# Transposing a value matrix and ternary feed-forward weights on VectorE instead of TensorE, in a graph layer on one Trainium2 core

## What is computed

```
xn = layernorm(x)
x  = x + segment_sum((xn @ W)[src] * edge_weight, dst) + mix(xn)
mix: q, k, v = xn @ Wq.T + bq, xn @ Wk.T + bk, xn @ Wv.T + bv      # q, k divided by their norms
     s = sum over m of phi(q) * phi(k), per head;  out = s * v / s
x  = x + ffn(layernorm(x))
ffn: act_quant(x) @ weight_quant(w_gate).T, the same with w_up, silu(gate) * up, then w_down
weight_quant(w): scale = 1 / mean(|w|);  wq = clip(round(w * scale), -1, 1) / scale
```

## Time and profile before

| what | us |
|---|---|
| median of 3 runs | 1679.87 |
| lowest and highest run | 1676.17, 1680.43 |
| the profiled execution's own time | 1680.37 |
| its span on the core | 1678.6 |
| TensorE busy in it | 1653.2 |
| VectorE busy | 1095.4 |
| ScalarE busy | 519.1 |
| GpSimd busy | 588.5 |

### The profile page before, as it was taken

One profiled execution on the slowest core, in us unless ns is written; L12 is line 12 of the kernel. 1 busy time (PEld: TensorE's weight loads), 2 busy tenths in 40 slices (PEclk: granted clock), 3 DMA queues, 4 the chain that ended last, 5 costly groups with the idle time before them and its releaser, 6 DMA issues.

```text
span 1678.6 us, 23146 instructions
## 1 busy us (share of the span) xinstructions
PE 1653.2 (98%) x8036; PEld 1344.9 (80%) x8036; DVE 1095.4 (65%) x2548; ACT 519.1 (31%) x618; POOL 588.5 (35%) x392
## 2 busy tenths in 40 slices
PE   6999999999999999999999999999999999999998
PEld 5899999888888888888877777888788887887665
DVE  7866573576676876656666664476485674764886
ACT  4632210222222111114232222233333333332554
POOL 2011565777776777777677700000000000000000
PEclk9999999999999999999999999999999999999999
DMA  9999878655676755657877747345345345452454
GB/s 295 377 402 348 308 234 263 169 138 124 151 195 167 183 141 149 149 138 191 243 209 192 191 147 205 102 135 137 96 146 136 96 136 145 136 145 62 146 172 123
DMA packets 158003, 302.93 MB, mean 180 GB/s; under 512 B 60241, under 2 KB 95105, under 8 KB 157938
## 3 DMA queue, kind: packets, MB, share of 16 engines
q1 hardware_dynamic: 88302, 222.54, 42.2%
q0 software_dynamic: 61824, 52.62, 15.3%
q10 hardware_dynamic: 7812, 26.97, 5.3%
HBM read 202.88 MB, written 99.20 MB: 180 GB/s over the span
## 4 chain that ended last, share of the span: by engine, by line
PE 91%; DMA 5%; DVE 2%; issue 1%; ACT 1%; SPq 0%; DVEq 0%; ACTq 0%
PE PS L367 23%; PE PS L368 23%; PE PS L366 23%; PE PS L1408 4%; PE PS L1410 4%; PE PS L1409 4%; PE PS L1645 4%; DMA Aside<-A_dense 2%; PE PS L1675 2%; PE PS L1472 2%; DMA xnT<-XT 1%; DMA X<-in_x 1%; PE PS L1624 1%; DVE stats L995 1%; PE PS L1388 0%
## 5 line engine op out<-in xcount | busy, mean ns | idle before, releaser
L706 POOL DMA_INDIRECT A_dense<-wtot,cell x336 | 545.4, 1623 | 229.5 <-DMA A_dense<-wtot,cell 133.9
L367 PE MATMUL PS<-SH,AL 125*125 125x512 f32 x784 | 310.0, 395 | 0.0
L366 PE MATMUL PS<-SL,AH 125*125 125x512 f32 x784 | 308.4, 393 | 1.6 <-DVE AL L1222 1.4
L368 PE MATMUL PS<-SH,AH 125*125 125x512 f32 x784 | 309.8, 395 | 0.0
L366 PE MATMUL PS<-WL,xtH 128*125 128x512 f32 x640 | 252.9, 395 | 0.0
L367 PE MATMUL PS<-WH,xtL 128*125 128x512 f32 x640 | 252.0, 394 | 0.0
L368 PE MATMUL PS<-WH,xtH 128*125 128x512 f32 x640 | 251.6, 393 | 0.0
L1220 DVE TENSOR_TENSOR SL<-S,SH 125x1024 fp32r<-125x1024 f32 x98 | 119.9, 1223 | 166.1 <-ACT SH L895 166.1
L895 ACT ACTIVATE SH<-S 125x1024 fp32r (+1 forms) x98 | 103.9, 1061 | 316.4 <-PE PS L368 316.3
L366 PEld LDWEIGHTS PS<-SL,AH 125*125 125x125 f32 x784 | 145.9, 186 | 39.8 <-DVE AL L1222 3.1
L367 PEld LDWEIGHTS PS<-SH,AL 125*125 125x125 f32 x784 | 146.1, 186 | 36.0
(11 more groups left out here) (190 smaller groups left out, 2547.9 us busy)
## 6 DMA issues: line engine op xcount, KB each, us to landing
A_dense<-zeros POOLq DMA_DIRECT2D x40, 1280.0 KB, 8.3
xt<-xnT SPq DMA_DIRECT2D x60, 500.0 KB, 6.1
Araw<-A_dense SPq DMA_DIRECT2D x100, 250.0 KB, 2.7
Aside<-A_dense SPq DMA_DIRECT2D x100, 250.0 KB, 2.9
keyrow<-key_rows SPq DMA_DIRECT2D x42, 512.0 KB, 4.1
ewrow<-weight_rows SPq DMA_DIRECT2D x42, 512.0 KB, 5.6
xnT<-XT ACTq DMA_DIRECT2D x20, 500.0 KB, 10.2
zx<-in_x SPq DMA_DIRECT2D x20, 448.0 KB
```

Of the source, the lines that this page charges most:

```text
L366: nc.tensor.matmul(o, lh, rl, start=start, stop=False)
L367: nc.tensor.matmul(o, ll, rh, start=False, stop=False)
L368: return nc.tensor.matmul(o, lh, rh, start=False, stop=stop)
L706: pool.indirect_dma_start(cells[m], bass.IndirectOffsetOnAxis(cell[:, col:col + 1], 0), wtot[:, col:col + 1], None, compute_op=ALU.add).th ...
```

## The change

Two transposes leave TensorE. VectorE's transpose works on blocks of 32 by 32, so a 128 by 128 transpose needs the blocks put in their places as well; here the access pattern of the instruction and the store to DRAM do that.

- **Wv.** In map tiles 10 to 17 DVE turns one block of Wv at the end of the tile (`turn_blocks`, into one buffer `turned`), and SP stores it with four DMAs of 32 partitions. ACT's copy is gone. wvT now holds column blocks instead of k-blocks, so W can no longer be replaced block by block: in the last source tiles TensorE makes the left half of the columns of both tiles, then the right halves (`half_products`), and the first two value tiles go in the same order. ACT and DVE replace four column blocks at a time.
- **Ternary weights.** The twelve chunks are quantised in the aggregation's group 0 instead of the value stage, in the places given by CHUNKS_AT (pair h of source tiles). The sums of |w| stay where they were. POOL's queue loads the chunks and stores them, eight DMAs of 32 partitions each, after the scatter is over. DVE turns the rounded chunk. SP reads wT in group 1 instead of group 0.
- The feed-forward matmuls read wT in 16 runs of 32 columns.
- EDGE_PLAN moves four pairs of edge columns from the map stage into the stage of Wq's and Wk's Gram matrices, and the scatter leaves out the three columns that hold no edge (333 instead of 336).

```diff
-EDGE_PLAN = [1] * TILES + [0, 0, 0, 0, 1, 1, 1, 1] + [0, 1, 1, 0, 1, 1, 0, 1] + [1, 0, 1, 0, 1, 0, 1, 1] \
-    + [1, 1, 1, 1, 1, 1, 0, 0] + [4] + [2] * KT + [3] * (TILES - KT) + [4] * 18 + [0] * 2
+EDGE_PLAN = [1] * TILES + [0, 0, 0, 0, 1, 1, 1, 1] + [0, 1, 1, 1, 1, 1, 0, 1] + [1] * KT \
+    + [1, 1, 1, 1, 1, 1, 0, 0] + [4] + [2] * KT + [3, 3] + [3, 2] * (KT // 2) + [3, 3] + [4] * 18 + [0] * 2
...
+CHUNKS_AT = (0, 0, 1, 1, 2, 1, 2, 1, 2, 2)
...
+    def across_blocks(ap):
+        return ap.rearrange("p (k b j) -> p b k j", b=4, j=32), lambda o: o.rearrange("p (b k j) -> p b k j", b=4, j=32)
+
+    def turn_blocks(out_, in_):
+        order_in, order_out = across_blocks(in_)
+        return nc.vector.transpose(order_out(out_), order_in)
...
+    def store_halves(eng, dram, rows, sem, down):
+        for a in range(4):
+            for c in range(2):
...
+                eng.dma_start(to, rows[a * 32:(a + 1) * 32, :].rearrange("p (b c f) -> p b c f", b=4, c=2)[:, :, c]).then_inc(sem, 16)
...
@@ sync @@
-        for f in range(3):
-            load_next_A(f + 2)
+        for hh in range(2, HALF + 2):
+            load_next_A(hh)
+        for f in range(3):
+            for i in range(2):
+                sp.wait_ge(s_fout[i], 128 * (2 * f + 2))
             sp.dma_start(wT[:, f], wT_d[4 * f:4 * f + 4].rearrange("c p n -> p c n")).then_inc(s_wT, 16)
+            load_next_A(HALF + 2 + f)
@@ gpsimd, behind the scatter @@
+        wait_stage4(pool)
+        for i in range(2):
+            pool.wait_ge(s_pe5[i], 1)
+        for c in range(2):
+            load_chunk(c)
+        for c in range(12):
+            if c + 2 < 12:
+                pool.wait_ge(s_fq16[c % 2], c // 2 + 1)
+                load_chunk(c + 2)
+            pool.wait_ge(s_fT[c % 2], c // 2 + 1)
+            store_halves(pool, wT_d[c], gTb[:, c % 2, :], s_fout[c % 2], c >= 8)
@@ scalar, in group 0 behind both source tiles of pair h @@
+            for c in range(chunk, chunk + CHUNKS_AT[h]):
+                act.wait_ge(s_fr[c % 2], c // 2 + 1)
+                if c >= 2:
+                    act.wait_ge(s_fT[c % 2], c // 2)
+                nc.scalar.activation(gqb[:, c % 2, :], gwb[:, c % 2, :], ACT.Identity, bias=neg_round[:, :]).then_inc(s_fq16[c % 2], 1)
@@ vector, map stage @@
+            j = t - V_TURN
+            if 0 <= j < KT:
+                dve.wait_ge(s_stage[j % 2], 32 + 16 * (KT // 2) + 16 * (j // 2) + 16)
+                if j:
+                    dve.wait_ge(s_vout, 64 * j)
+                turn_blocks(turned[:, :], stage[:, j % 2, :]).then_inc(s_vtr, 1)
@@ vector, group 0 @@
+            low_of_sources(2 * h, 0, h)
+            for c in range(chunk, chunk + CHUNKS_AT[h]):
...
+            low_of_sources(2 * h + 1, 1, h)
+            for c in range(chunk, chunk + CHUNKS_AT[h]):
+                i = c % 2
+                dve.wait_ge(s_fq16[i], c // 2 + 1)
+                if c >= 2:
+                    dve.wait_ge(s_fout[i], c // 2 * 128)
+                turn_blocks(gTb[:, i, :], gqb[:, i, :]).then_inc(s_fT[i], 1)
@@ tensor @@
-                for e in range(8):
-                    last = nc.tensor.transpose(PS16[:, 6 + i, e * P:(e + 1) * P], fqb[:, i, e * P:(e + 1) * P], ident16[:, :])
-                last.then_inc(s_ftr[i], 1)
...
+        pe.wait_ge(s_vl, KT // 2)
+        for i in range(2):
+            pe.wait_ge(s_xtl[i], 2 * HALF + 1)
+            pe.wait_ge(s_supev[i], HALF)
+            half_products(i, 0)
+        pe.wait_ge(s_vl, KT)
+        for i in range(2):
+            half_products(i, 1).then_inc(s_mm[i], 1)
...
+        def up_blocks(c, k):
+            return wT[:, c, :, :].rearrange("p q (a k j) -> p (q a) k j", a=4, j=32)[:, :, k, :]
```

More of the change, by code:

```diff
@@ L94 @@
 END_AT = 229368
+CHUNKS_AT = (0, 0, 1, 1, 2, 1, 2, 1, 2, 2)
+assert len(CHUNKS_AT) == HALF and sum(CHUNKS_AT) == 12
 def split_rows(eng, dst, src, sem):
@@ L590, in stage4_tile @@
                 load_next_A(0)
-            if chunk is None and isinstance(h, int) and t < 6:
+            if t < 5:
                 for a in range(2):
@@ L703, in scatter_pair @@
             turns[m] += 1
-            for c in range(2):
-                col = 2 * pair + c
+            for col in range(2 * pair, min(2 * pair + 2, COLS)):
+                c = col % 2
                 pool.indirect_dma_start(cells[m], bass.IndirectOffsetOnAxis(cell[:, col:col + 1], 0),
@@ L861, in _ @@
         high_of_tile(1, HALF - 1 + PASS)
+        act.wait_ge(s_wk, 1)
+        for j in range(KT // 2):
+            high_of_block(j)
         sources_out(HALF - 1, 0)
         high_of_tile(0, HALF + PASS)
[L865 to L871 removed]
@@ L917, in _ @@
         act.wait_ge(s_mm[1], 3 * HALF)
-        with act.Fori(1, HALF) as h:
+        chunk = 0
+        for h in range(1, HALF):
             high_of_pair(0, h)
+            for c in range(chunk, chunk + CHUNKS_AT[h]):
[3 more added lines that the diff above has]
+                nc.scalar.activation(gqb[:, c % 2, :], gwb[:, c % 2, :], ACT.Identity, bias=neg_round[:, :]).then_inc(s_fq16[c % 2], 1)
+            chunk += CHUNKS_AT[h]
         def move_rows(g):
@@ L1287, in _ @@
         stage4_tile(9, 1)
-        with dve.Fori(1, HALF) as h:
-            low_of_pair(0, h)
+        dve.wait_ge(s_fc, 3)
+        chunk = 0
+        for h in range(1, HALF):
+            low_of_sources(2 * h, 0, h)
+            for c in range(chunk, chunk + CHUNKS_AT[h]):
+                i, f = c % 2, c // 4
+                dve.wait_ge(s_gw[i], c // 2 * 16 + 16)
+                nc.vector.tensor_scalar(gwb[:, i, :], gwb[:, i, :], wq_sc[:, f:f + 1, 1], 1.0,
+                                        ALU.mult, ALU.min).then_inc(s_fm, 1)
+                dve.wait_ge(s_fm, c + 1)
+                nc.vector.tensor_scalar(gwb[:, i, :], gwb[:, i, :], -1.0, ROUND, ALU.max, ALU.add).then_inc(s_fr[i], 1)
+            low_of_sources(2 * h + 1, 1, h)
[5 more added lines that the diff above has]
+                turn_blocks(gTb[:, i, :], gqb[:, i, :]).then_inc(s_fT[i], 1)
+            chunk += CHUNKS_AT[h]
         with dve.Fori(1, GROUPS) as g:
@@ L1546, in _ @@
             pe.wait_ge(s_supev[i], HALF - 1)
-            source_tile(HALF - 1, i, used=s_wk if i else None)
+            pe.wait_ge(s_xtl[i], HALF + PASS)
+            last = half_products(i, 0)
+        last.then_inc(s_wk, 1)
+        for i in range(2):
+            half_products(i, 1).then_inc(s_mm[i], 1)
+        pe.wait_ge(s_vl, KT // 2)
         for i in range(2):
@@ L1551, in _ @@
             pe.wait_ge(s_supev[i], HALF)
-            tile_products(i, WH, WL, ready=s_vl if i == 0 else None)
+            half_products(i, 0)
+        pe.wait_ge(s_vl, KT)
+        for i in range(2):
+            half_products(i, 1).then_inc(s_mm[i], 1)
         with pe.Fori(1, 3) as h:
```

206 lines of the change are left out of this document (101 added, 105 removed).

## The result

The changed kernel takes 1703.0 us (median of 4 runs, 1702.0 to 1704.7), the kernel before 1678.0 (4 runs, 1676.0 to 1680.4) beside it: ratio 1.015, interval 1.0137 to 1.0163. The forecast was 1672 in a range of 1666 to 1684. The profiled execution took 1703.5 us with a span of 1701.5, 22.9 more than the span of 1678.6 before.

The account below looks back on a forecast made before the run. TensorE's own instructions were taken to bound the kernel all the way; -13.2 + 1.5 + 3.5 - 1.2 + 1.5 = -7.9 from 1680.4 gave 1672.5, stated as 1672 us. The eight-in-ten range was 1666 to 1684.

Parts of the forecast that it names:

- Source to value stage: First value tiles made by halves: TensorE waits 1.2 us for VectorE at value tile 2; taken +1.5, bounds 0 and 4.
- My rival on the slower side: Group 0: POOL's queue becomes the bound, VectorE's transposes wait for stores; 27 us at the pace 1.2, so 1696; chance 0.14.
- What leaves TensorE: Transposes gone from TensorE: 6.9 us for eight Wv blocks, 6.3 us for twelve ternary chunks, together -13.2 us.
- Map stage: VectorE's Wv transpose, taken at 1.2 us, fits its idle time; cost 0, up to +2 where a load comes late.
- Group 0: TensorE waits 3 us for low part 19, behind chunk 11's late load; with lengthened issues, +3.5.
- D: Pace of POOL's DMA issues in group 0: 0.75 us chosen, between 0.5 and 1.85.
- L: Landing time of a chunk's load in group 0: 3.8 us taken, between 2.9 and 6.2.
- 9 D + L - 7.6: TensorE's wait for low part 19 in group 0, from nine POOL issues, a landing and 7.6 us of slack: 3 us.
- Roundings beside the queue: VectorE's roundings lengthen POOL's issues by up to 0.7 us; at 0.3 each, 0.5 us more wait in group 0.
- Loads: In group 0, wT's first third comes later, so a late adjacency block costs less: -1.2, bounds -1.6 and +1.
- The collision in group 1: wT's first third meets the write of r, partly behind an already late adjacency block: +1.5, bounds 0 to 4.
- Moving operand in short runs: Last stage: 480 matmuls reading runs of 32 columns cost 0, bounds 0 and +7; the slower case had chance 0.06.

Follow-up runs that it names:

- e5: The changed kernel with ScalarE's |w| sums ahead of the high half and the total of the sums behind value tile 7: 1670.7 us, ratio 0.9952.
- e6: e5 with GpSimd's queue issuing both weight loads of a two-chunk step ahead of its sixteen stores: 1665.6 us, ratio 0.9927.
- e11: e6 run again unchanged, as partner for later kernels: 1668.0 us, ratio 0.9936.
- e1: The changed kernel with ScalarE's |w| sums of value tile t (0 to 5) ahead of the high half of tile t+2: 1675.0 us, ratio 0.9975.
- e9: e6 without the Wv part, so Wv is transposed by TensorE as in the kernel before: 1672.6 us, ratio 0.9968.
- e3: The kernel before with only ScalarE's new order, the high half of value tile t+2 ahead of tile t's sums: 1711.9 us, ratio 1.0189.

## Why the prediction was wrong

- **Source to value stage: the step that failed.** I costed it at +1.5, with bounds of 0 and 4, from VectorE's operations alone. It measured 34.1 us. I wrote that the sums stayed where they were; they did, and the instruction ahead of them on the same engine didn't. ScalarE's high half had moved one tile forward, and its waits became the sums' waits. ScalarE's busy share of 31% said nothing of it: the order matters, and I had not followed who waits for the sums (SyncE's queue, with z, x and xt behind). None of my rivals had it. My rival on the slower side had GpSimd's queue in group 0, and the kernel was slower for another reason.
- **The halves themselves:** without the ring and the early total, value tiles 1 to 6 take 58.6 to 58.9 us (e5, e6, e11) against 55.5 before: about 1.2 us at tile 2, as worked out from the earlier trace rows, and some 2 more up to tile 6. Inside the bounds, above the 1.5 that I took.
- **What leaves TensorE:** 7.0 us in the map stage (forecast 6.9). Eleven of the twelve chunks stood behind value tile 7, which starts at 868.4 instead of 842.3; from there to group 0 the changed kernel gains 26.1 - 20.1 = 6.0 us, and about 0.5 in tile 6 (forecast 6.3 for twelve).
- **Map stage:** 0, as costed. VectorE's transpose takes 1.23 us (I took 1.2):

```profile
L416 DVE STREAM_TRANSPOSE gTb<-gqb x12: 1200/1238/1246, 1038.8 to 1123.5; 128x1024 bf16<-128x1024 bf16 x12
L416 DVE STREAM_TRANSPOSE turned<-stage x8: 1229/1233/1241, 440.0 to 516.0; 128x1024 f32<-128x1024 f32 x8
```

- **Group 0:** +3.5 forecast, 2.6 measured to the start of group 1. The place was right (the load of chunk 11, low part 19 behind it), the size came by luck: D was 0.549 us and not 0.75, and L 1118.57 - 1112.84 = 5.7 us and not 3.8. In 9 D + L - 7.6 the two errors cancel: 3.0 forecast, 3.0 by the measured values. And TensorE didn't wait 3.0 us for low part 19 but 1.6, so the term of 7.6 was too small as well; one source tile later came 0.6 us more, for `zr`, which VectorE then had to add late and which I had not counted.

```profile
L430 POOL DMA_DIRECT2D ternary<-gTb x96: 549/549/739, 1040.4 to 1132.0; - x96
```

- **Roundings beside the queue:** the longest of the 96 stores took 739 ns against the median of 549; in e6 the longest took 992 ns, and the sixteen stores beside the roundings of chunks 10 and 11 took 9.75 us where the last sixteen, with none beside them, took 8.69. So single issues are lengthened, by 0.1 to 0.44 us, and the mean hardly (96 stores in 52.6 us, 0.548 each). The Trainium skill (SBUF — State Buffer, "SBUF: two separate sides") has descriptor writes locked out while such an operation runs; the trace agrees with that. Each store over 0.6 us (4 of the 96, 9 in e6) ends 0.12 us behind the end of one of VectorE's two rounding operations; one that began 0.2 us or more ahead of the operation kept its 0.55. What failed is my sum from it, a D of 0.91: I added each rounding's whole 1.46 us, but an issue does part of its own work in that time (1.06 us lost over two roundings in e6), and many roundings met an idle queue.
- **Loads:** the -1.2 did not come in the changed kernel. There wT's first third had gone to group 1, and an adjacency block still came 5.69 us late (VectorE's addition at 1045.76), with TensorE 1.3 us late behind it, as before. So the third was not the cause, or not alone; the load of zr still stands ahead of that block. In e1 TensorE lost 1.0 us at this place, in e5 0.3, in e6 and e9 nothing, in e11, which is e6 again, 0.2. None of these edits touches the place, and no run was made to tell what moves it. The collision in group 1 (+1.5) hardly came: that group took 112.0 us against 111.6.
- **Moving operand in short runs:** 0, as taken. Against the earlier trace rows:

```profile
L1723 PE MATMUL PS<-wT,rqT 128*125 128x512 bf16 x320 | 75.0, 379 | 0.0
```

The sum then closes: up to the map stage -2.8, transposes -7.0, ring and halves +34.1, tile 6 +1.8 (2.3 for the low clock less the 0.5 of its chunk), the other chunks -6.0, group 0 +2.6, the rest of the aggregation 0, last stage +0.2: +22.9. The first, -2.8, is no part of the change that I can name. Between profiled executions the map stage starts anywhere from 308.7 to 313.9 us, and the two kernels with the latest starts are before and e3; no run here was made to tell why. With e1's 4.4 in place of the 34.1 and no low clock in tile 6 the same sum is -9.1, and -6.3 without the start, where I had forecast -7.9. The timed runs of e1 give less, 4.4 us under the kernel before (2.5 to 6.0 by the interval). So even with the ring open the forecast was too good: value tiles 1 to 6 cost 4.4 us and not 1.5, and of the 1.2 us of the loads most did not come. But these are small beside the one wait that I had not followed, and that decided.

## What to carry to other kernels

When a diff moves an instruction on any engine, even one by one place, write down what it waits for and what is queued behind it, and follow those who wait for these around until the path ends or comes back. A path that comes back has a period; compare that with the bottleneck's tile, not the engine's busy share. Put what a queue needs soon (sums, loads) ahead of what waits for a fresh load, and place a small join on the critical engine as late as its result allows: here these two orders and one on the DMA queue turned 1.5% slower into 0.6 to 0.7% faster (e6, and e11 again), the best kernel of the study.

## What the runs showed of the hardware

- A plain DMA of 128 pieces from GpSimd's queue is issued in 0.549 us, a third of an indirect one of as many (1.54).
- VectorE's 32 by 32 transpose of 128x1024 takes the same 1.23 us in fp32 and bf16.
- In the changed kernel a z store directly behind two weight loads of 512 KB had landed, so that the load of x could go out, 6.0 and 6.8 us after its issue (779.02 to 785.04, 794.93 to 801.72); before, with the loads six microseconds ahead of it, it was 4.0 (791.70 to 795.72).
- A store issued from GpSimd's queue beside one of VectorE's rounding operations ended 0.12 us behind that operation's end, in all 13 cases of two traces where it took over 0.6 us instead of 0.55.
- TensorE's clock stayed low behind the wait of 17 us: value tile 6 took 13.4 us (855.0 to 868.4) instead of 11.1, so the wait cost about 2.3 us beyond itself.
